# Two-layer transformer on one core: in layer one's attention, both query halves go together and GpSimd adds probability blocks before the ones matmuls

## The reference

```python
q = (x @ wq.T).reshape(b, t, NUM_HEADS, 2, HEAD_DIM)     # 16 heads, 2 halves of 16 dims
k = (x @ wk.T).reshape(b, t, NUM_HEADS, 2, HEAD_DIM)
v = (x @ wv.T).reshape(b, t, NUM_HEADS, 2 * HEAD_DIM)
attn1 = softmax(q1 @ k1.T * scale) @ v                    # no mask in this layer
attn2 = softmax(q2 @ k2.T * scale) @ v
attn = attn1 - lambda_full * attn2
attn = attn * rsqrt(mean(attn * attn) + EPS) * subln_w * (1.0 - LAMBDA_INIT)
return attn @ wo.T
```

## Time and profile before

| what | value |
|---|---|
| three timed runs | 2406.16, 2409.13, 2413.46 us (median 2409.13) |
| the profiled execution | 2410.03 us, its span 2408.3 us |
| granted TensorE clock, mean over the span | 0.983 |
| layer one's heads, first round to last reduce | 177.9 to 1021.2 us of the span |
| one head of layer one in the middle of it | 26.2 us |
| the feed-forward net, second attention and last layer | the rest |

### The profile page before, as it was taken

One profiled execution on the slowest core, in us unless ns is written; L12 is line 12 of the kernel. 1 busy time (PEld: TensorE's weight loads), 2 busy tenths in 40 slices (PEclk: granted clock), 3 DMA queues, 4 the chain that ended last, 5 costly groups with the idle time before them and its releaser, 6 DMA issues. The chain is left out here.

```text
span 2408.3 us, 43565 instructions
## 1 busy us (share of the span) xinstructions
PE 2324.1 (97%) x15600; PEld 1328.4 (55%) x15600; DVE 1626.7 (68%) x3789; ACT 1231.6 (51%) x2454; POOL 260.5 (11%) x412
## 2 busy tenths in 40 slices
PE   6999999999999999999999999988899999999989
PEld 5663333333333333377888888876644444444477
DVE  2347888888888888374444444453379898888667
ACT  3126766776776676642212212243156676666734
POOL 4000000000100000050000000002012212112152
PEclk9999999999999999999999999998899999999999
DMA  5653322222322200002000000002632122220011
GB/s 194 158 143 63 96 28 28 28 28 39 43 28 28 28 2 2 4 29 70 27 27 27 26 26 24 2 1 77 143 57 42 28 37 42 42 42 3 2 40 57
DMA packets 58285, 109.09 MB, mean 45 GB/s; under 512 B 11820, under 2 KB 23084, under 8 KB 58088
## 3 DMA queue, kind: packets, MB, share of 16 engines
q1 hardware_dynamic: 56776, 101.30, 20.5%
q0 software_dynamic: 1312, 5.24, 0.6%
HBM read 73.75 MB, written 31.46 MB: 44 GB/s over the span
## 5 line engine op out<-in xcount | busy, mean ns | idle before, releaser
L612 ACT ACTIVATE l_w_hi_prob<-l_p_work 128x512 f32<-128x512 f32 (+3 forms) x1792 | 871.1, 553 | 350.7 <-PE l_p_work L504 333.6
L669 DVE TENSOR_REDUCE l_maxima<-l_p_ring 128x1 f32<-128x512 f32 x1280 | 806.3, 683 | 129.4 <-PE l_p_ring L482 120.4
L524 PE MATMUL l_p_work<-l_w_hi_prob,v_all 128*32 128x512 f32 (+3 forms) x3584 | 805.7, 556 | 0.6 <-ACT l_w_hi_sums L592 0.2
L524 PE MATMUL l_p_work<-l_w_hi_prob,l_ones 128*32 128x512 f32 (+3 forms) x3584 | 805.7, 556 | 0.0
L504 PE MATMUL l_p_work<-xT_all 50*128 50x512 f32 (+3 forms) x1680 | 427.6, 409 | 0.0
L482 PE MATMUL l_p_ring<-xT_all 48*128 48x512 f32 (+3 forms) x1680 | 427.5, 411 | 0.0
L482 PEld LDWEIGHTS l_p_ring<-xT_all 48*128 48x128 f32 x1680 | 216.5, 185 | 234.2 <-DVE l_maxima L669 155.8
L524 PEld LDWEIGHTS l_p_work<-l_w_hi_prob,v_all 128*32 128x32 f32 x3584 | 166.4, 109 | 318.2 <-issue 201.6
L504 PEld LDWEIGHTS l_p_work<-xT_all 50*128 50x128 f32 x1680 | 221.9, 185 | 162.4 <-ACT l_w_hi_prob L612 114.2
L666 DVE CUSTOM_DVE_ANT_0 l_masked_scores<-l_p_ring,l_mask 128x128 bf16<-128x128 f32 (+3 forms) x512 | 235.4, 486 | 50.5 <-PE l_p_ring L482 45.1
L1212 DVE SCALAR_TENSOR_TENSOR ffn_h<-ffn_p_u,ffn_group_scales,ffn_silu 128x512 f32<-128x512 f32 x64 | 48.0, 751 | 205.4 <-PE ffn_p_u L228 194.5
(11 more groups left out here) (153 smaller groups left out, 3058.2 us busy)
## 6 DMA issues: line engine op xcount, KB each, us to landing
xT_all<-q_parts SPq DMA_DIRECT2D x180, 128.0 KB
q_parts<-l_part SPq DMA_DIRECT2D x64, 256.0 KB
xT_all<-k_parts SPq DMA_DIRECT2D x90, 128.0 KB
k_parts<-l_part SPq DMA_DIRECT2D x40, 256.0 KB
xT_all<-k_parts SPq DMA_DIRECT2D x90, 64.0 KB
x<-in_x_T SPq DMA_DIRECT2D x4, 1024.0 KB, 11.1
x<-in_L_attn_x POOLq DMA_DIRECT2D x1, 4096.0 KB, 14.8
ffn_w<-in_L_ffn_gate_w_T SPq DMA_DIRECT2D x8, 512.0 KB, 3.6
```

Of the source, the lines that this page charges most:

```text
L524: summing = pe.matmul(p_out[r0:r0 + VD, off:CH], lhs, prob[step % PRING][:, sub, off:CH], start=first, stop=final)
L612: act.activation(prob[step % PRING][:, sub, off:CH], p_score[:, at % SCORE_BANKS, off:CH], ACT.Exp, scale=HD ** -0.5).then_inc(exped, 1)
L669: dve.tensor_reduce(to, scores, AX.X, ALU.max).then_inc(freed, 1)
```

## The change

Layer one's attention only (`self.joint`, true where the layer isn't causal):

- The steps of a head go over the key blocks outermost and over both query halves inside (`for kt ... for qc`). A round of `sum_values` now takes one key block: four matmuls, v against 2 subs times 2 query halves, 8 rounds for each head. They accumulate in `p_out`.
- The denominators have rounds of their own (`sum_ones`): four matmuls of ones, again 2 subs times 2 query halves, into the bank `p_ring[RING - 1]`. The ring for maxima, shift and turn has 3 banks instead of 4 in this layer.
- For key blocks 0 to 5, GpSimd first adds two blocks (`add_pair`, one `tensor_tensor` of 128x1024 for each query half, 6 for each head) into one of three rooms, the `part` buffers of the projections; one ones round then serves two key blocks. Key blocks 6 and 7 are taken as they are. This makes `ONES_ROUNDS` = 5, and 13 rounds for each head instead of 16.
- `prob` has 8 slots instead of 4. The four new ones lie in the room of x, between `early_q` and `early_k`. So only half of the residual x is loaded after head 1 (4 DMAs), and the other half at the start of `mix_phase`, by 4 DMAs at the head of SyncE's queue; VectorE waits for them after its first reciprocal.
- Values and denominators are copied, turned and kept together once for each head (`copy_values`, `copy_ones`, two turns, `keep_joint`). The mean of squares comes two heads later than before on VectorE.
- The pattern of layer one is new, with D for a ones round.

The core of the diff:

```diff
+JOINT_PRING = 8
+PAIRED = 3
+ONES_ROUNDS = PAIRED + KT - 2 * PAIRED
+ONES_BEHIND = 2
...
+        self.joint = not causal
+        self.ring = RING - 1 if self.joint else RING
+        self.prob_ring = JOINT_PRING if self.joint else PRING
+        if self.joint:
+            self.steps = [(qc, kt, 0) for kt in range(KT) for qc in range(QC)]
...
-L0 = Layer("l0", D, D, False, "VUQWWPRSUWRQVQVVWRQRUUQWUUURRQWQURSQWWXURUVRQWUVRQVQWWRVRQSWWQVSPTTRVSWWWVQR",
-           24, (4, 3))
+L0 = Layer("l0", D, D, False, "QDRUQUURDQURUQWRUQURWUQURQUDRQUUURWUQRUUQWXUURUDQUURWUQRQUUWTWRUUUQRWUQRUDQURUU",
+           24, (3, 11))
...
+        p_ones = p_ring[:, RING - 1, :]
+        pairs = [room[:, :, :].bitcast(F32) for room in part_room]
...
+            def add_pair(n, s):
+                i = pair_index(n, s)
+                room, step = i % PART_BUFFERS, n * S + s
+                if i < PART_BUFFERS:
+                    pool.wait_ge(stored[room], 16 * PARTS * len(range(room, L.units, PART_BUFFERS)))
+                else:
+                    m, p = divmod((i - PART_BUFFERS) // QC, PAIRED)
+                    pool.wait_ge(ones_summed, m * ONES_ROUNDS + p + 1)
+                pool.wait_ge(exped, 2 * (step + 1))
+                pool.tensor_tensor(pairs[room], prob[(step - QC) % L.prob_ring][:, :, :], prob[step % L.prob_ring][:, :, :],
+                                   ALU.add).then_inc(paired, 1)
...
-                if L.bank_at[item] >= RING:
-                    pe.wait_ge(freed, L.bank_at[item] - RING + 1)
+                if L.bank_at[item] >= L.ring:
+                    pe.wait_ge(freed, L.bank_at[item] - L.ring + 1)
...
+            def sum_values(n, kt):
+                if n == kt == 0:
+                    pe.wait_ge(v_kept, NT)
+                if n and kt == 0:
+                    pe.wait_ge(out_copied, n)
+                pe.wait_ge(exped, 2 * (n * S + QC * (kt + 1)))
+                tile, col = L.v_column(n)
+                v = v_sb[:, (tile + kt) * L.v_dims + col:(tile + kt) * L.v_dims + col + VD]
+                for sub in range(2):
+                    for qc in range(QC):
+                        r0 = (2 * sub + qc) * VD
+                        summing = pe.matmul(p_out[r0:r0 + VD, :], v, prob[(n * S + QC * kt + qc) % L.prob_ring][:, sub, :],
+                                            start=kt == 0, stop=kt == KT - 1)
+                summing.then_inc(summed, 1)
+
+            def sum_ones(n, p):
+                if n and p == 0:
+                    pe.wait_ge(ones_copied, n)
+                kt = 2 * PAIRED + p - PAIRED
+                if p < PAIRED:
+                    pe.wait_ge(paired, QC * (n * PAIRED + p + 1))
+                else:
+                    pe.wait_ge(exped, 2 * (n * S + QC * (kt + 1)))
...
+                        summing = pe.matmul(p_ones[r0:r0 + VD, :], ones[:, :], added[:, sub, :],
+                                            start=p == 0, stop=p == ONES_ROUNDS - 1)
+                summing.then_inc(ones_summed, 1)
...
+                if step >= L.prob_ring and L.joint:
+                    m, older = divmod(step - L.prob_ring, S)
+                    act.wait_ge(summed, m * KT + L.steps[older][1] + 1)
+                    kt = L.steps[older][1]
+                    if kt < 2 * PAIRED:
+                        act.wait_ge(paired, pair_index(m, older) + 1)
+                    else:
+                        act.wait_ge(ones_summed, m * ONES_ROUNDS + kt - PAIRED + 1)
...
+            def keep_joint(n):
+                dve.wait_ge(filled, L.filled_at["turn", n, 1])
...
+                dve.reciprocal(recip[:, :, :, 0], ones_at[:, :, :, 0]).then_inc(out_recip, 1)
...
+                dve.tensor_tensor(half[:, :, :, :].rearrange("p j b w -> p b j w"), values, recip[:, :, :, :].to_broadcast([P, QPC, 4, VD]),
+                                  ALU.mult).then_inc(freed, 2)
...
+                dve.scalar_tensor_tensor(
+                    out=to, in0=half[:, 2:4, :, :].rearrange("p q b w -> p (q b) w"), scalar=neg_lambda,
+                    in1=half[:, 0:2, :, :].rearrange("p q b w -> p (q b) w"), op0=ALU.mult, op1=ALU.add).then_inc(out_kept, 1)
...
@@ mix_phase @@
+            for dst, src in rows:
+                sp.dma_start(dst, src).then_inc(rows_in, 16)
...
             dve.reciprocal(inv_rms[:, :, :], inv_rms[:, :, :]).then_inc(inverted, 1)
+            if rows:
+                dve.wait_ge(rows_in, 16 * len(rows))
```

More of the change, by code:

```diff
@@ L148, in heads @@
         S, U = len(self.steps), len(self.pairs)
-        done = {"score": [SUM_LAG] * 2, "maxima": [self.first_pairs] * 2, "sum": 0, "shift": 1}
-        out, turns = [("score", *divmod(i, S), sub) for i in range(SUM_LAG) for sub in range(2)], []
+        ahead = SUM_LAG * (QC if self.joint else 1)
+        done = {"score": [ahead] * 2, "maxima": [self.first_pairs] * 2, "sum": 0, "ones": 0, "shift": 1}
+        out, turns = [("score", *divmod(i, S), sub) for i in range(ahead) for sub in range(2)], []
+        first_skipped = ONES_BEHIND
         def take(name, size, sub):
@@ L577, in _ @@
                     score(*at)
+                elif what == "sum" and L.joint:
+                    sum_values(*at)
+                elif what == "ones":
+                    sum_ones(*at)
                 elif what == "sum":
@@ L742, in _ @@
                         average(at[0] - 1)
-            average(HEADS - 1)
+            for n in range(HEADS - 3 if L.joint else HEADS - 1, HEADS):
+                average(n)
 def tile_pipeline(engine, *stages, written_out=WRITTEN_OUT):
```

142 lines of the change are left out of this document (106 added, 36 removed).

## The result

The changed kernel takes 2373.49 us (median of four runs, 2366.85 to 2376.99) beside 2411.3 us of the kernel before on the same chip: ratio 0.984 (95% interval 0.981 to 0.987), 38 us faster. The forecast was 2372, 2355 to 2400. Its profiled execution is the quickest of the four, 2366.85 us, with a span of 2364.9.

A forecast was written before the change was run, and what follows sets the result against it. TensorE's own work was taken to bound each head, VectorE next. Start 0.7 + 29 heads x 1.3 + tail 1.8 - mix 2.5 = 37.7 us off 2410.0 gave 2372 us, range 2355 to 2400.

The forecast's parts named there:

- The bound: In the heads before, TensorE's own work sets the 26.20 us; VectorE is next, 3.6 us below.
- Rounds: TensorE in a head: 16 rounds at 15.1 us become 13 lone ones at 1.00 us each, 2.1 us less.
- Batches: TensorE's score and maxima batches: one fewer at 0.95 us, two more at 0.69, +0.43 us a head.
- The ring: Three banks make late maxima wait in some six batches (7 to 12): 0.4 us a head, between 0 and 0.9.
- The start: Head 1's first scores stay at 203.21 us behind queued shift rows; shift 2 comes 0.7 us earlier.
- VectorE: In a head, two keeps (1.95 us) become one joint keep (1.39): VectorE 22.1 us, below the head's 24.9.
- GpSimd: Six adds a head of 2.1 to 2.6 us, 15.5 us in all, hidden until one add takes about 3.9 us.
- Tail and mix: Behind shift 31 the attention's end gains 1.8 us; at the mix VectorE waits for x, losing 2.5 us.
- Four different moving operands: Rival in the rounds: four moving operands cost more than two, a round up to twice; chance 0.03.
- Held VectorE: Rival: the joint keep's last instruction waits up to 2.6 us for an add; time 2381 to 2410 us; chance 0.10.
- Tighter ring: Rival: a late bank costs 0.15 us in every batch; heads 25.6 to 25.9 us, time about 2395; chance 0.14.

The follow-up runs named there:

- E11: The changed kernel run and profiled once more, without edits: median 2374.12 us, ratio 0.9839 to the kernel before, heads of 24.63 us.
- E6: Changed kernel with GpSimd's adds over 32 of 512 columns only: heads of 24.63 us, GpSimd busy for 1.94 us of them instead of 14.26.
- E3: Changed kernel with row maxima over only the first 256 of each 512 keys: heads of 24.31 us instead of 24.63.
- E1: Kernel before with three instead of four banks in the maxima ring, nothing else: shift 0 at 150.8 us, heads of 28.67 us, total 2493.6 us.
- E2: Changed kernel with four ring banks up to the last projection, three from the first head on: shift 0 at 145.7 us, heads of 24.63 us.
- E7: Changed kernel with VectorE waiting for x only at its first add in the mix: first split 7.3 us after the last mean of squares, not 8.7 to 9.1.
- E10: Changed kernel with four banks up to the first head and VectorE's wait for x at its first add: 2361.93 us, ratio 0.9805 to the kernel before.
- E5: Changed kernel with each GpSimd add done twice, 12 instead of 6 a head: heads of 32.75 us, total 2625 us.
- E4: Changed kernel's joint order without GpSimd's adds, 16 rounds instead of 13: heads of 27.50 us, total 2454.5 us.

## Why the prediction was right, step by step

The time (2372 against 2373.5) is better than its parts, and its closeness is luck: errors stood against each other. The heads gave 8 us more than forecast, the start 6.6 less in the first profile and 12.2 less in the second (E11, whose 2374.60 us is nearer the median). Behind the feed-forward net the first profile won 4 us more and the second 1 us, which the forecast didn't have either.

- **The bound.** TensorE's own work, then VectorE: right. E6 shows that GpSimd's part is free, E3 that VectorE matters by 0.32 us only.
- **Rounds.** 13 at 1.00 us: measured 0.996 for values and ones. Four different moving operands cost nothing; that rival is out.
- **Batches.** A term that was mis-sized, by 0.2 us a head: +0.43 forecast, +0.25 measured (eleven batches of 9.9 us before, twelve of 10.1 in E3). The 0.95 us of the earlier trace rows was not the usual price: of the ten batches of six in that head before, seven took 0.90 or 0.91 and three 0.95 or 0.96. The forecast's sentence that no batch of before shows a wait passed over these three; what they lost their 0.05 us to is open. TensorE's own head is 24.31 and not 24.5.
- **The ring.** 0.32 against 0.4 in the heads, in the batches named (1.01, 1.01 and 1.03 or 1.04 us, batches 7, 9 and 11). The head came to 24.62 instead of 24.9, 29 x 0.28 = 8.1 us more than forecast.
- **The start, the step that failed.** "That stays, and what was won before it is lost": I put the first scores of head 1 at 203 us, because their shift rows are queued behind DMAs, and looked at the ring only in the heads. The projections use the same ring. They lost 6.4 us by shift 0 (E1, E2), the DMAs came late with them, and head 1 started at 210.23 (212.27 in E11). From there to shift 2 it took 17.06 us, 17.5 forecast; but that agreement is luck too. In the five other profiles with this order and three couples, E2, E6, E7, E10 and E11, it took 19.5 to 20.6, with 5.4 to 8.0 us of it at half clock, for which the forecast has no term. Shift 2 was 5.9 late (11.5 in E11) instead of 0.7 early: -6.6 us (-12.2).
- **VectorE.** The joint keep took 0.26 + 0.69 + 0.49 = 1.43 (1.39). VectorE's head is 22.53 and not 22.1. Of the 0.4, 0.24 are the reduces, which are busy for 20.19 us instead of 19.95; the rest I haven't separated. It isn't the adds (22.54 in E6).
- **GpSimd.** 2.38 us an add (between 2.1 and 2.6), 14.26 a head (15.5), with cover as reckoned. With adds twice as long, beyond the threshold of 3.9 us, GpSimd's loop is the bound (E5).
- **Tail and mix.** +1.9 (+1.8) and -2.2 (-2.5). VectorE's wait in the mix is confirmed by E7 for 1.4 to 1.9 us of it.
- **The rivals.** Held VectorE: the mechanism exists (1.47 against 0.48), the place was free, as argued. Tighter ring: not in this order, but 2.5 us a head in the old one; I weighed the ring by a loop of this order only and didn't see how much the order did.

## What to carry to other kernels

When a change takes a buffer away, walk through every stage that uses the ring, not only the one that the change is about: the loss was in the projections, where the consumer waits for a store. Profile a kernel twice before pricing a repair by one pair of profiles: here the same kernel reached shift 2 at 227.3 and at 232.9. When a table sets the order of TensorE, price a batch by its fuller half and check that each batch pairs its halves, before counting rounds saved. And a time that comes out right says little of its terms; read the places (shift 0, shift 2, shift 31, the first split of the mix) one by one.

## What the runs showed of the hardware

- Matmuls of this kernel on the two halves of the rows go side by side; in 33 of 38 batches the fuller half gives the time: 0.43, 0.67, 0.90, 1.13 us for 1 to 4.
- A VectorE instruction with two SBUF inputs that starts during a GpSimd add lasts until 0.28 or 0.29 us behind the add's end (22 of 22 in E5, 1.47 instead of 0.48 us in the one shown), while VectorE's reduces from PSUM beside 14.26 us of adds a head take the same 684 ns as beside 1.94.
- At head 1's first scores TensorE waits for a transfer. Behind waits of 2.9 to 5.1 us (eleven profiles and the one of before) it was granted half clock for 3 us and more; behind 1.5 us (changed kernel, first profile) and 0.4 us (E4) it was not. In every profile of the changed kernel's order it had also worked at half clock for 10 us or more in head 0. So one kernel's start came out 5.6 us apart in two profiles.
